# Where the residual x is added, and when the Wv folding is done, in a two-attention transformer layer

## The reference

```python
xn = layernorm(x)                                # over the width
q, k, v = xn @ Wq.T, xn @ Wk.T, xn @ Wv.T        # first attention, 16 heads of 128
q, k = rope(q), rope(k)
s = causal((q @ k.T) ** 4)
attn1 = (s @ v) / max(sum(s), 1e-6) @ Wo.T
# second block, on hidden = xn
h1 = rmsnorm(hidden) * ln1_w
attn2 = softmax_attention(h1) @ Wo2.T            # used only in
mod = 0.1 * tanh(attn2 @ A)                      # A is 2048 x 16
h2 = rmsnorm(hidden) * ln2_w
gate = silu(h2 @ W_in.T + mod * (h2 @ A) @ B)
ffn = hidden + (gate * (h2 @ W_up.T)) @ W_down.T
out = x + attn1 + ffn
```

## Time and profile before

| what | value |
|---|---|
| median of 3 runs (lowest to highest) | 5578.88 us (5363.6 to 6134.32) |
| profiled execution | 5360.49 us |
| its span on the slowest core, on the fastest | 5358.6 us, 5343.9 us |
| Wo1 stage on the slowest core | from about 1364 to 1809 us |
| second attention | from about 1870 to 2680 us |
| FFN | from about 2700 us to the end |
| busy share of the span: PE, DVE, ACT, POOL | 91%, 27%, 24%, 14% |

### The profile page before, as it was taken

One profiled execution on the slowest core, in us unless ns is written; L12 is line 12 of the kernel. 1 busy time (PEld: TensorE's weight loads), 2 busy tenths in 40 slices (PEclk: granted clock), 3 DMA queues, 4 the chain that ended last, 5 costly groups with the idle time before them and its releaser, 6 DMA issues.

```text
span 5358.6 us, 66244 instructions; the slowest of 8 cores (5343.9 to 5358.6 us)
## 1 busy us (share of the span) xinstructions
PE 4869.0 (91%) x24000; PEld 2298.8 (43%) x24000; DVE 1446.9 (27%) x2132; ACT 1297.1 (24%) x2435; POOL 764.2 (14%) x1258
## 2 busy tenths in 40 slices
PE   5798998888755699999899999999999999999999
PEld 1354554444322344444344444444444444444444
DVE  5755555554333333334200000001101000000000
ACT  4345554455100065656500000000000000000000
POOL 4411111111000133333200000000000000000000
PEclk8899999999877799999999999999999999999999
DMA  6221111112444211111244444456654444444554
GB/s 173 72 36 30 31 29 24 32 32 62 101 112 102 67 21 24 21 35 33 39 76 75 73 78 72 76 96 126 129 110 75 74 76 71 78 73 83 116 116 91
DMA packets 140802, 380.47 MB, mean 71 GB/s; under 512 B 15756, under 2 KB 32780, under 8 KB 139848
## 3 DMA queue, kind: packets, MB, share of 16 engines
q0 software_dynamic: 74896, 269.06, 31.1%
q1 hardware_dynamic: 65304, 105.09, 6.1%
q10 hardware_dynamic: 288, 2.10, 0.1%
HBM read 603.18 MB, written 42.03 MB: 120 GB/s over the span
## 4 chain that ended last, share of the span: by engine, by line
PE 77%; DVE 10%; DMA 6%; issue 4%; ACT 1%; POOL 1%; SPq 0%; DVEq 0%; ACTq 0%; POOLq 0%
PE ps L249 77%; DMA xt<-xt 5%; DVE xt L252 2%; DVE tr L252 2%; DVE xf L252 1%; DVE ps L252 1%; DVE sa L252 1%; DMA xf<-xt 1%; POOL sa L252 0%; SPq L75 0%; DVE arm L262 0%; ACT pt L265 0%; POOL qs L252 0%; DVEq L100 0%; ACT sa L265 0%
## 5 line engine op out<-in xcount | busy, mean ns | idle before, releaser
L249 PE MATMUL ps<-hh,w 128*128 128x512 bf16 x8192 | 1808.9, 379 | 1.3 <-ACT sgt L265 1.3
L249 PEld LDWEIGHTS ps<-hh,w 128*128 128x128 bf16 x8192 | 801.4, 98 | 968.3 <-issue 2.2
L249 PE MATMUL ps<-xn,w 128*128 128x512 bf16 x4096 | 1168.4, 384 | 34.7 <-POOL xn L252 34.7
L249 PE MATMUL ps<-gu,w 128*128 128x512 bf16 x4096 | 884.4, 379 | 0.0
L265 ACT ACTIVATE sgt<-ps 128x512 f32<-128x512 f32 x256 | 152.9, 597 | 2123.7 <-PE ps L249 2117.8
L252 DVE TENSOR_TENSOR gu<-sgt,ps 128x512 bf16<-128x512 f32 x256 | 176.1, 688 | 1649.7 <-ACT sgt L265 1649.7
L249 PEld LDWEIGHTS ps<-gu,w 128*128 128x128 bf16 x4096 | 400.8, 98 | 483.3
L249 PEld LDWEIGHTS ps<-xn,w 128*128 128x128 bf16 x4096 | 397.0, 99 | 464.4 <-issue 59.7
L265 ACT ACTIVATE pt<-ps,negb 128x512 bf16<-128x512 f32 (+3 forms) x640 | 383.7, 624 | 273.6 <-PE ps L249 271.0
L265 ACT ACTIVATE z<-ps 128x512 f32<-128x512 f32 (+3 forms) x640 | 336.3, 531 | 410.2 <-PE ps L249 311.1
L249 PE MATMUL ps<-ao,w 128*128 128x512 bf16 x1024 | 266.9, 419 | 126.5 <-DVE xt L252 126.5
(11 more groups left out here) (114 smaller groups left out, 2989.3 us busy)
## 6 DMA issues: line engine op xcount, KB each, us to landing
w<-wint POOLq DMA_DIRECT2D x128, 512.0 KB, 5.1
w<-wupt POOLq DMA_DIRECT2D x128, 512.0 KB, 5.2
w<-wdnt POOLq DMA_DIRECT2D x128, 512.0 KB, 6.4
xf<-xt SPq DMA_DIRECT2D x16, 1024.0 KB, 16.3
xt<-xt SPq DMA_DIRECT2D x64, 256.0 KB, 3.8
base_sp<-xt SPq DMA_DIRECT2D x64, 256.0 KB, 2.2
ob<-base_sp SPq DMA_DIRECT2D x64, 256.0 KB, 5.0
outt<-ob SPq DMA_DIRECT2D x64, 256.0 KB, 5.0
```

What stands on the lines that cost most here:

```text
L249: return lambda e: e.matmul(out, lhsT, rhs, start=st, stop=en)
```

## The change

Three things, all in how the code emits the work; the arithmetic is the same up to the order of the sum.

- `wo1_group` no longer loads x. DVE makes one operation of it, PSUM minus MREP, and the piece is stored. x * (1 + rs) is added in the second attention: at every fifth tile of heads 0 to 8, `residual_load` issues the loads of a piece of x (`RX`) and of the stored piece (`RB`) on SP, and `residual_add` issues for the piece before it two DVE operations and the store back to `base_sp`. There are 64 pieces and two buffers of each kind. Loading the rows for h2 moves from the start of head 8 to its second query block, and waits for the last two pieces.
- `prep_wva` is a filler of the first attention, behind `prep_woa` of the same head; both run one head later than `prep_woa` did. Its result `WVA` has to live through the first attention, and now lies over the weight slots 4 and 5. The ring has 4 slots until V' is made, and 6 again from then on.
- `wo1_early` takes 3 output tiles in place of 5, so that the Wo1 stage has 61 groups in place of 59.

```diff
-        WVA = at("wva", 4096, BF16, O_A + 16 * KB)
+        WVA = at("wva", 4096, BF16, O_W + 16 * KB)
+        RX = [at(f"rx{i}", 512, F32, O_A + (16 + 2 * i) * KB) for i in range(2)]
+        RB = [at(f"rb{i}", 512, F32, O_A + (20 + 2 * i) * KB) for i in range(2)]
...
-            plan(("wo2", h), din["wo2t"][h])
-        for ic in range(5):
+            for g in ([h - 1] if h else []) + ([h] if h == H - 1 else []):
+                plan(("wo2", g), din["wo2t"][g])
+                plan(("wv2", g), din["wv2t"][g])
+        for ic in range(16):
             plan(("wo1", ic), din["wo1t"][ic])
-        for ic in range(16):
-            if ic >= 5:
-                plan(("wo1", ic), din["wo1t"][ic])
-            plan(("wv2", ic), din["wv2t"][ic])
...
-        for slot in range(5):
+        for slot in range(4):
             wload(slot, None)
...
+        def prep_wva(h):
...
+            wload(slot, tok)
+            t_wva[h] = P.dve(cp(WVA[:].rearrange("p (j c) -> p j c", j=NJ)[:, :, h * 16:(h + 1) * 16],
+                                ps[bank][:, 0:256].rearrange("p (j c) -> p j c", j=NJ)),
+                             [tok, qk_last[0]])
...
-            tl = P.dma("sp", f"xt{n}", xt[:], xT[ic * 128:(ic + 1) * 128, cs], first)
...
-            a = P.dve(tt(xt[:], xt[:], AREP[:, cs], ALU.mult), [tl, rep["a"]])
-            a = P.dve(tt(xt[:], xt[:], MREP[:, cs], ALU.subtract), [a, rep["m"]])
-            a = P.dve(tt(xt[:], ps[bank][:], xt[:], ALU.add), [a, tok])
+            a = P.dve(tt(xt[:], ps[bank][:], MREP[:, cs], ALU.subtract), [tok, rep["m"], first])
...
-                    if h == 1:
-                        wload(5, qk_last[0])
                     if h + 1 < H:
                         fillers.append(fill_first(h + 1))
-                        rate = (266 if (h + 1) % 2 == 0 else 136) / PER_HEAD
+                        rate = (272 if (h + 1) % 2 == 0 else 142) / PER_HEAD
                     else:
-                        rate = 90 / PER_HEAD
-                    fillers.append(prep_woa(h))
+                        rate = 106 / PER_HEAD
+                    for g in ([h - 1] if h else []) + ([h] if h == H - 1 else []):
+                        fillers.append(prep_woa(g))
+                        fillers.append(prep_wva(g))
...
+        wload(4, tok)
+        wload(5, tok)
...
+        def residual_load():
+            n = len(rdone) + len(rpend)
+            r = n % 2
+            ic, tb = rlist[n]
+            tx = P.dma("sp", f"rx{r}", RX[r][:], xT[ic * 128:(ic + 1) * 128, tb * 512:(tb + 1) * 512],
+                       [rfree[r], t_k[H - 1, NTB - 1], vfree[0], vfree[2]])
+            tb_ = P.dma("sp", f"rb{r}", RB[r][:], base_sp[ic, tb], [rfree[r], t_base[ic, tb]])
+            rpend.append((ic, tb, r, tx, tb_))
+
+        def residual_add():
+            ic, tb, r, tx, tb_ = rpend.pop(0)
+            a = P.dve(tt(RX[r][:], RX[r][:], AREP[:, tb * 512:(tb + 1) * 512], ALU.mult), [tx, rep["a"]])
+            a = P.dve(tt(RB[r][:], RB[r][:], RX[r][:], ALU.add), [a, tb_])
+            t_base[ic, tb] = rfree[r] = P.dma("sp", f"rb{r}", base_sp[ic, tb], RB[r][:], [a])
+            rdone.append(t_base[ic, tb])
...
+                if i % 5 == 0 and h < 9:
+                    if len(rdone) + len(rpend) < len(rlist):
+                        residual_load()
+                        if len(rpend) == 2:
+                            residual_add()
```

More of the change, by code:

```diff
@@ L525, in prep_woa @@
             yield 0.4
+        t_wva = {}
+        def prep_wva(h):
+            slot, wt = wget("wv2", h)
+            bank = next_bank()
+            tok = None
+            for jc in range(NJ):
+                tok = P.pe(mm(ps[bank][:, jc * 16:(jc + 1) * 16], W[slot][:, jc * 128:(jc + 1) * 128],
+                              WOA[:, h * 16:(h + 1) * 16], True, True),
+                           [wt, t_woa[h]] + ([free[bank]] if jc == 0 else []), inc=(jc == NJ - 1))
+                if jc < NJ - 1:
+                    yield 0.4
+            wload(slot, tok)
+            t_wva[h] = P.dve(cp(WVA[:].rearrange("p (j c) -> p j c", j=NJ)[:, :, h * 16:(h + 1) * 16],
+                                ps[bank][:, 0:256].rearrange("p (j c) -> p j c", j=NJ)),
+                             [tok, qk_last[0]])
+            free[bank] = t_wva[h]
+            yield 0.4
+        qk_last = {}
         fillers = []
@@ L603, in build @@
         t_ao = {}
-        qk_last = {}
         rows_all = [t_rows[tb] for tb in range(NTB)]
@@ L703, in wo1_early @@
         def wo1_early():
-            for ic in range(5):
+            for ic in range(3):
                 held[ic] = wget("wo1", ic)
@@ L738, in to_h1 @@
                              [rep["rsh"], t_l1, last_proj["t"]] + [t_xsp[tb, jc] for tb in range(NTB)])
[L740 to L754, removed]
         FB[:] = [0, 1, 2, 3, 4, 5, 6, 7]
@@ L759, in build @@
         for ic in range(16):
-            if ic >= 5:
+            if ic >= 3:
                 held[ic] = wget("wo1", ic)
             box = {}
-            for tb in range(1 if ic < 5 else 0, NTB):
+            for tb in range(1 if ic < 3 else 0, NTB):
                 run(wo1_group(ic, tb, *held[ic], 4, box))
             wload(held[ic][0], box["t"])
-            prep_wva(ic)
             to_h1(ic)
@@ L930, in h2_piece @@
             t_h2[hf, jc, i] = t
-        hwait = [vp_all, t_h1[NJ - 1], wo1_last["t"]]
+        rlist = [(ic, tb) for ic in range(16) for tb in range(NTB)]
+        rpend = []
+        rfree = [None, None]
+        rdone = []
+        def residual_load():
[12 more added lines that the diff above has]
+            rdone.append(t_base[ic, tb])
+        hwait = [vp_all, t_h1[NJ - 1], wo1_last["t"], rep["a"]]
         rt0 = []
@@ L942, in build @@
                         rate2 = 138 / PER_HEAD
-                if h == 8 and qb == 0 and t == 0:
+                if i % 5 == 0 and h < 9:
[3 more added lines that the diff above has]
+                            residual_add()
+                    elif rpend:
+                        residual_add()
+                        hwait = hwait + rdone[-2:]
+                if h == 8 and qb == 1 and t == 0:
                     rt0 = h2_rows(0, hwait)
```

## The result

| | before | after |
|---|---|---|
| lowest and highest of 4 runs | 5357.4, 6134.3 us | 5150.6, 5200.8 us |
| median of 4 runs | 5471.2 us | 5154.6 us |
| profiled execution, its span | 5360.5, 5358.6 us | 5154.4, 5152.8 us |
| spans of the 8 cores | 5343.9 to 5358.6 us | 5134.9 to 5152.8 us |

The change makes the kernel faster: ratio 0.9636, interval 0.9542 to 0.9729, against the runs of before beside it. In some executions the cores of one die, or of both, run at a lower granted clock and take some per cent longer; the upper part of the spread of before, with the 5578.9 that was the median at the prediction, is of that kind, and the comparison leaves such executions out.

What follows compares the result with a forecast made beforehand. A chain of waits, in the Wo1 stage SP's load, DVE and store loop, was taken as the bound. Terms -231.6 + 2 + 15 + 5 + 5 = -204.6 took 5360.5 to 5156 us; range 5112 to 5232.

Steps and rivals of the forecast that it cites:

- Sum: Whole kernel: terms add to -204.6, so 5360.5 becomes 5156 us, set against the profiled execution, not the 5578.9 median.
- The Wo1 stage: Between first attention and V': without x loads and two DVE operations, PE is the bound; 231.6 us saved.
- The 3.5 us set aside for the clock and the tail: Wo1 stage allowance: 1.5 us for V' waiting on the last scaled tile, 2 for the clock.
- The prep of Wv2 leaves the stage, no gain of its own: Wo1 stage: the prep moves out, but PE was waiting there anyway, so no separate gain.
- the clock stays low: Rival, Wo1 stage: PE at 1.2 GHz, stage 421 us, kernel 5363; chance 0.05 shared with a chain near its limit.
- the rival that stores hold the loop: Rival, Wo1 stage: stores as slow as loads would make the stage gain less; no separate chance given.
- The last head: End of first attention: two groups move out, the AREP wait stays, fewer filler matmuls; +2 us, from -8 to +8.
- The first attention, ring of 4: Late q weights make PE wait 2.2 us at 7 head boundaries; +15 us, from below 0 to 51.
- The folding: First attention: added matmuls mostly hide, waits for DVE copies grow; +5 us for 16 heads, from 0 to 30.
- The second attention: Residual's DVE operations and transfers laid over its heads mostly fit beside existing work; +5 us, from 0 to 40.
- The rival's 89 us: Second attention: DVE and POOL block each other, 64 x 1.4 us lost, giving 5240; band 5190 to 5250, chance 0.18.
- One sign of being wrong: Second attention: heads 0 to 8 longer than heads 9 to 15 would show the forecast wrong.

Runs made afterwards that it cites:

- order alone: Kernel before, with SP issuing each Wo1-stage load of x two groups ahead and nothing removed: 5167.9, 5169.6, 5172.1 us, ratio 0.9645.
- the fold alone: Changed kernel with the x loads and three DVE operations back in the Wo1 stage and no residual step in the second attention: 5357.8 us, ratio 1.0004.
- the residual part alone: Kernel before with only the residual moved to the second attention; Wv2 folding stays in the Wo1 stage, ring keeps 6 slots: 5134.1 and 5134.5 us, ratio 0.9579.
- before with 4 slots: Kernel before with a ring of 4 slots and 3 early output tiles, folding still in the Wo1 stage: 5370.1 us in one run.
- prep first: Changed kernel with prep_woa and prep_wva, and their weights, ahead of the projections in odd heads: 5129.5, 5132.2, 5133.6 us, ratio 0.9581.
- the run with DVE only: Changed kernel with only the residual's two DVE operations left in the second attention, on AREP, without loads or stores: 5147.4 us in one run.

## Why the prediction was right, and where it was not

**The base was the step that failed.** The measured time, 5154.6, is 1.4 us from the 5156 predicted. But the median that was shown was 5578.9, and against it 5156 reads as a gain of 7.6%; the measured one is 3.6%. In "Sum" I wrote that this median stood 4% above the profiled execution, "which no row of this profile explains", and left it at that: 218 us, more than the whole gain, got no term and no rival. The runs showed in its place that the median is not what this kernel takes: its lowest was 5357.4, 5354.6 and 5354.2 in the three sets of runs beside the experiments, and of the 13 runs of the first set eight lie within 5357.4 and 5365.6. The profiled 5360.5 lies among them, and the gain should have been stated as 204.6 of it, 3.8%, in so many words.

**The Wo1 stage** (-231.6; measured -235.1). Right, with its cause: order alone takes 186 to 193 us off it, core by core. The 3.5 us set aside for the clock and the tail were hardly needed: the clock is 1.00, and V' waits 1.6 us once. "The prep of Wv2 leaves the stage, no gain of its own" held too: the fold alone has ratio 1.0004. The rival "the clock stays low" is out: with the waits gone the same stage ran at 1.00. So is the rival that stores hold the loop: with all its 61 stores the stage runs at PE's pace.

**The last head** (+2, from -8 to +8; measured -8.6 on core 4, -10.3 on core 0). Outside its bounds. Two groups moved out, 6.9 us. That DVE no longer waits there for x was named but given no price: with the residual part alone and the same groups, head 15 takes 54 us in place of 59.5. The 5.93 us behind the AREP row, which "stays", are gone from PE's waits; in their place PE waits for weights, which the term did not have (core 4, 1334.7 to 1386 us):

```profile
PE ps L252 <- DMA w<-wv2t: 3.9, 1, 3.9
PE ps L252 <- DMA w<-wo1t: 3.7, 1, 3.7
```

**The first attention, ring of 4** (+15, "the first q matmul of heads 2, 4, to 14 waits 2 us"). Place right, price wrong in both its parts. On core 4 from 226 us on, and on core 0:

```profile
PE ps L252 <- DMA w<-wq1t: 7.1, 5, 1.7
```
```profile
PE ps L252 <- DMA w<-wq1t: 0.2, 1, 0.2
```

The wait is 1.4 us in the mean, not 2.2, and only some cores have it: 4.7 to 7.1 us in all on cores 1, 2, 4 and 6, and 0.2 to 0.7 on the others. The timeline of PE on core 4 where the q projection begins, 6.9 us after its issue:

```profile
362.45 0.59 PE L252 MATMUL ps<-xn,w 128*128 128x512 bf16 x2 [1.60 <-DMA w<-wq1t]
...
363.32 1.06 PE L252 MATMUL ps<-xn,w 128*128 128x512 bf16 x2
```

and the same place on core 0, where the tile had landed:

```profile
354.55 0.59 PE L252 MATMUL ps<-xn,w 128*128 128x512 bf16 x2
...
355.31 0.59 PE L252 MATMUL ps<-xn,w 128*128 128x512 bf16 x2
```

Behind the wait the same pair of matmuls takes 1.06 us in place of 0.59: PE has fallen to 1.2 GHz. Core 4 ended head 0 6.3 us behind core 0 (286.8 and 280.5) and ends head 1 9.6 us behind (369.8 and 360.2), so this place cost 3.3 us for a wait of 1.6. But such a fall is not tied to the q weights. On core 5, with 0.5 us of these waits in all, it stands behind a wait for POOL:

```profile
369.75 0.22 PE L252 MATMUL ps<-sa,v 128*128 128x128 bf16 x1 [2.19 <-POOL sa L255]
...
369.87 1.06 PE L252 MATMUL ps<-xn,w 128*128 128x512 bf16 x2
```

Heads 1 to 14 of before (core 0), and of the changed kernel on core 0 and on core 4, in the columns of the earlier trace rows:

```profile
284.30:1306.60 1022.30, 914.88 (x5475) 504.20 (x5472) 536.86 (x851) 516.85 (x1066) 135.31 (x281) 0.99 0.18 31
280.50:1316.20 1035.70, 926.72 (x5723) 513.84 (x5721) 542.72 (x865) 519.45 (x1066) 143.72 (x295) 0.99 0.21 38
286.80:1334.70 1047.90, 925.71 (x5613) 515.53 (x5720) 542.57 (x866) 519.89 (x1066) 144.04 (x295) 0.98 0.21 37
```

By the clock records of these traces, PE was granted 1.2 GHz for 10.2, 23.9 and 37.5 us of them, and on core 5 for 37.5. If half of that time is lost, which is an estimate from the 1.06 against 0.59 us above, the clock costs 7 us more than before on core 0 and 14 on core 4; the q weights cost 0.2 and 7.1, and the waits for the WOA copy 5.5 more on both (19.0 in place of 13.5). That makes 13 and 26, where 13.4 and 25.6 were measured; the added matmuls, and smaller changes of other waits in both directions, are not in it, so the sum is an account and no proof. So of the +15 for the q weights up to half came true, on half of the cores, and the term that was missing in the sum is the clock, in heads whose PE is partly idle, behind whatever wait. I named the ring of 4 as the cause of the late q weights; it is the order of the list with that ring, since either a shorter list (before with 4 slots) or another order (prep first) has no such wait.

**The folding** (+5, from 0 to 30). Inside its range, but too small. On core 0, where the q weights cost nothing, heads 1 to 14 are 13.4 us longer; 5.5 of it are the waits for the WOA copy, and up to 7 the clock. That the first attention ends where it did before when the prep comes first does not show the work to be free, since that order removed another wait as well.

**The second attention** (+5, from 0 to 40; measured +9.4). Inside the range, and both mechanisms named are seen: POOL's masks are longer beside the new DVE operations, and the loads are sometimes late. The rival's 89 us assumed that POOL is held for the full 1.4 us of each pair; POOL worked 16 us more in all (258.1 in place of 241.9). One sign of being wrong was met, in small: heads 1 to 7, with the residual, take 50.1 us each, and heads 9 to 14 48.6, before 48.8.

```profile
DVE rx L255 <- DMA rx<-xt: 21.2, 18, 2.4
```

The chain was costed with 2.5 us to spare in 12.2, and held: the longest wait is 2.4, and `rx` landed in 3.7 us in the median, 7.7 at worst, not the 14.1 from which the kernel would have been slower. What I did not have is that the two together cost more than the two apart. PE's waits in this stretch grew for the masks (5.0 to 7.6 us) and for `pt` of ACT (17.6 to 19.2) and fell for the squares (30.2 to 28.2), 2 us in all. The clock accounts for more, by the same estimate: PE was granted 1.2 GHz for 13.7 us of this stretch before (core 0) and for 23.9 after (core 4), at most 5 us of loss; and in the run with DVE only, the cores with 17.1 us of it take 731.5, those with 20.5 or 23.9 take 733.2. Why it fell more often is not shown, and some 2 us stay open. "The FFN is unchanged" was right.

## What to carry to other kernels

Where a load and a store alternate on one issuing queue and the store waits for an engine, the load is bound to that engine's pace, here with four buffers; look at the order of the queue before the amounts, and try first to issue the loads ahead. Extra work is free only where it meets neither a full engine nor a narrow chain: the same residual cost 10 to 13 us in the attention, with its POOL masks and chains through three engines, and nothing in the FFN. Of a weight ring, ask which tile of the list is needed first after a stall of the list. Where TensorE is partly idle, look at its granted clock before and after a change, also where no wait is new. And before a gain is stated, settle which time of the kernel it is a share of.

## What the runs showed of the hardware

- Waits of TensorE of 1.6 us, for a transfer (core 4), and of 2.2 us, for POOL (core 5), were each followed by matmuls at half clock within 1 us. PE had been partly idle before both; that the wait alone did it is not shown.
- In heads 1 to 14 of the first attention, where PE is busy for nine tenths, the time at 1.2 GHz was 6.8 to 10.2 us on the eight cores before and 20.5 to 44.4 after, with at most 7.1 us of new waits for weights. In the FFN all eight cores had 1.00 from 2600 to 3300 us.
- 256 KB loads of x landed in 3.2 us (median, with stores) at a DMA share of 0.47 and in 6.2 at 0.81, in the same stage of two kernels. DVE still waited 71.4 us for them at 189 GB/s, with the loads issued two groups ahead.
- DVE operations on two SBUF float32 inputs lengthened POOL's masks from 429 to 514 ns in the mean and its squares from 1041 to 1175; transfers of the same pieces did not (425, 1042).
